# Expert outputs of a decoder layer added straight into the output tensor, with other tokens' rows for the spare places of a slot

## The reference, cut to what matters

```python
x = x + self_attention(layernorm(x))
x = x + cross_attention(layernorm(x), ctx)
# ffn on h = layernorm(x)
probs = softmax(h @ classifier_w.T)                 # 12 choices: 8 experts and 4 that return h
_, idx = top_k(probs + bias, 2)                     # two choices per token
rw = take_along_axis(probs, idx) * 1.5
for e in range(8):
    out += rw_e * ((silu(h @ gate_w[e].T) * (h @ up_w[e].T)) @ down_w[e].T)
out += h * sum(rw of the four others)
x = x + out
```

## Time and profile before

| what | us |
|---|---|
| median of 3 runs (2280.91 to 2284.15) | 2281.41 |
| the profiled execution, its own time | 2280.95 |
| its span, first to last instruction | 2279.2 |
| PE busy in the span | 2100.5 |
| DVE, ACT, POOL busy in the span | 1380.0, 946.2, 868.6 |
| 35 slots of `experts`, first instruction about 2027, to the end of the span | 252 |

### The profile page before, as it was taken

The page is one execution under the profiler, slowest core; times in us unless marked ns, Lnnn a source line. Parts: engine busy times, 40 slices in busy tenths (PEclk is TensorE's granted clock), DMA queues, the critical chain, the costliest instruction groups (busy, mean ns, idle before and its releaser), DMA issues. The chain is left out here.

```text
span 2279.2 us, 36906 instructions
## 1 busy us (share of the span) xinstructions
PE 2100.5 (92%) x10838; PEld 1693.3 (74%) x10839; DVE 1380.0 (61%) x3046; ACT 946.2 (42%) x2030; POOL 868.6 (38%) x977
## 2 busy tenths in 40 slices
PE   6899999987899997799999999999999799949994
PEld 6788888875777776588888888888887588824442
DVE  6455555557888886477677777777777556631110
ACT  4233333334232322365665665666565422213331
POOL 5100000002666666444433433443443256524552
PEclk9999999998999998899999999999999899969997
DMA  8212121146444444242222222222221284425555
GB/s 242 73 54 74 56 71 57 54 126 189 142 149 137 143 150 150 93 132 73 64 72 76 63 70 65 63 65 70 63 64 41 67 262 146 142 82 112 90 90 110
DMA packets 290938, 230.23 MB, mean 101 GB/s; under 512 B 150194, under 2 KB 257314, under 8 KB 288482
## 3 DMA queue, kind: packets, MB, share of 16 engines
q1 hardware_dynamic: 277122, 194.39, 29.0%
q0 software_dynamic: 8736, 18.39, 4.7%
q10 hardware_dynamic: 4992, 16.37, 2.2%
HBM read 140.30 MB, written 92.46 MB: 102 GB/s over the span
## 5 line engine op out<-in xcount | busy, mean ns | idle before, releaser
L2434 ACT ACTIVATE ca_prob<-ca_ps_s,ca_down,ca_scales 112x487 f32<-112x487 f32 x256 | 194.0, 758 | 243.2 <-DVE ca_down L2562 243.2
L2243 POOL TENSOR_TENSOR ca_k<-ca_k 125x512 f32<-125x512 f32 x64 | 83.1, 1298 | 326.1 <-DVE ca_k L2525 326.1
L2558 DVE TENSOR_REDUCE ca_top<-ca_ps_s 112x1 f32<-112x487 f32 x256 | 168.4, 658 | 42.6 <-PE ca_ps_s L77 42.6
L76 PE MATMUL out_ps_y<-out_w_lo,out_o_hi 128*128 128x512 f32 x448 | 178.6, 399 | 0.0
L645 POOL COPY sa_val<-lat_v 112x128 f32<-112x128 f32 (+1 forms) x64 | 19.6, 308 | 411.6 <-PE sa_ps_o L704 411.3
L75 PE MATMUL ca_ps_p<-ca_w_hi,ca_c_hi 128*125 128x512 f32 x384 | 157.2, 409 | 14.6 <-DVE ca_w_lo L2579 10.0
L75 PE MATMUL out_ps_y<-out_w_hi,out_o_hi 128*128 128x512 f32 x308 | 128.6, 418 | 37.9 <-DVE out_o_lo L1300 17.1
L2552 DVE TENSOR_TENSOR ca_pT_lo<-ca_ps_t,ca_pT_hi 125x448 fp32r<-125x448 f32 x256 | 152.7, 616 | 3.0 <-ACT ca_pT_hi L2442 3.0
L77 PE MATMUL ca_ps_p<-ca_w_hi,ca_c_lo 128*125 128x512 f32 x384 | 152.9, 398 | 0.0
L76 PE MATMUL ca_ps_p<-ca_w_lo,ca_c_hi 128*125 128x512 f32 x384 | 152.8, 398 | 0.0
L2333 PEld LDWEIGHTS ca_ps_t<-ca_ident,ca_prob 112*125 112x125 f32 x1024 | 132.3, 189 | 19.1 <-ACT ca_prob L2434 11.3
(11 more groups left out here) (299 smaller groups left out, 6074.1 us busy)
## 6 DMA issues: line engine op xcount, KB each, us to landing
self_outT<-sa_ov SPq DMA_DIRECT2D x64, 224.0 KB, 2.4
out_o_raw<-self_outT SPq DMA_DIRECT2D x56, 256.0 KB, 2.9
cross_qT<-out_qt SPq DMA_DIRECT2D x56, 256.0 KB, 2.4
ca_q_raw<-cross_qT SPq DMA_DIRECT2D x64, 224.0 KB, 2.8
cross_outT<-ca_ov SPq DMA_DIRECT2D x64, 224.0 KB, 3.0
out_o_raw<-cross_outT SPq DMA_DIRECT2D x56, 256.0 KB, 4.1
expert_raw<-in_expert_w SPq DMA_DIRECT2D x8, 1536.0 KB
ca_c_first<-in_ctxT SPq DMA_DIRECT2D x15, 750.0 KB, 5.2
```

The source lines that it names most:

```text
L76: pe.matmul(out, a_hi, b_lo, start=False, stop=False)
L2243: pool.tensor_tensor(k1[0:m, :], k1[0:m, :], k2[0:m, :], ALU.add).then_inc(k_added.sem, 1)
L2434: act.activation(prob[j % 2][:, 0:KV], ps_s[j % 2][:, 0:KV], ACT.Exp, bias=down[:, j:j + 1], scale=scales[par][:, n:n + 1], accum_out=tota ...
L2558: dve.tensor_reduce(top[:, j:j + 1], ps_s[j % 2][:, 0:KV], AX.X, ALU.max, negate=True).then_inc(topped.sem, 1)
```

## The change

The adds go straight to the output tensor `out`, where `cross_output` now also stores its rows. `rows_x`, its spare rows and the copy at the end are gone. `out` has no spare rows, so each spare place of a slot needs a real row that the slot doesn't hold (its addend is zero, but two addends of one DMA may not share a row). The numbers of these rows are computed per slot: DVE writes a 128x128 matrix of marks (`mark`, three instructions, for slot i+3 in step i), PE multiplies it with a column of ones into a new PSUM bank `ps_n` (in `turn_x`), and DVE turns the sums into row numbers (`name`, three instructions, for slot i+1 in step i, right behind `gate` of slot i). POOL's second conversion reads those numbers and waits for them. `turn_x` of slot n now waits for the marks of slot n and for the first instruction of `name` of slot n-1, since both use the one bank. `ps_a` gives up its second bank for it. Before the slots, POOL and DVE write seven small constants. On DVE, `name` of slot 0 stands behind `merge` of slot 4.

```diff
@@ cross_output, SP
-            sp.dma_start(rows_x[T:T + P, :], ahead_of.w_hi[:, 0, :].bitcast(F32)).then_inc(spare_put, 16)
...
-            sp.wait_ge(spare_put, 32)
+            sp.wait_ge(spare_put, 16)
@@ experts
-        ps_a = [ctx.bank(f"ps_a{i}", P, KI, P) for i in range(2)]
+        ps_a = ctx.bank("ps_a", P, KI, P)
+        ps_n = ctx.bank("ps_n", P, 1)
@@ SP
-            whole = lambda ap: ap.rearrange("(p n) d -> p (n d)", p=P)
             sp.wait_ge(put.sem, put.at(NU - 1))
-            sp.dma_start(whole(out), whole(rows_x[0:T, :])).then_inc(stored, 16)
-            sp.wait_ge(stored, 16)
@@ POOL
+            pool.iota(row_no_i[:, :], pattern=[[1, P]], base=0, channel_multiplier=0).then_inc(numbers, 1)
+            pool.iota(part_no_i[:, :], pattern=[[0, 1]], base=0, channel_multiplier=1).then_inc(numbers, 1)
+            pool.memset(ones[:, :], 1.0).then_inc(numbers, 1)
...
-                pool.tensor_copy(spot_i[i % 2][:, :], list_i[:, bass.ds(s, 1), 0]).then_inc(spotted.sem, 1)
+                wait(pool, named, s, 2)
+                carry(pool, h, ticks)
+                pool.tensor_copy(spot_i[i % 2][:, :], spot_f[:, bass.ds(s, 1)]).then_inc(spotted.sem, 1)
...
-                pool.indirect_dma_start(rows_x, bass.IndirectOffsetOnAxis(ap=spot_i[i % 2][:, 0:1], axis=0),
+                pool.indirect_dma_start(out, bass.IndirectOffsetOnAxis(ap=spot_i[i % 2][:, 0:1], axis=0),
@@ PE, turn_x
                 mm.then_inc(x_turned.sem, 1)
+                wait(pe, marked, n, 2)
+                if not isinstance(n, int) or n:
+                    wait(pe, named, n, -3)
+                pe.matmul(ps_n[:, :], missing[i % 4][:, :], ones[:, :], start=True, stop=True).then_inc(ranked.sem, 1)
@@ PE, turn
-                wait(pe, a_kept, n, -2)
+                wait(pe, a_kept, n, -1)
@@ DVE
+            def mark(h, i):
+                s = h * 4 + i
+                wait(dve, merged, s, 1)
+                carry(dve, h, ticks)
+                dve.tensor_copy(token[i % 4][:, :], list_i[:, bass.ds(s, 1), 0]).then_inc(marked.sem, 1)
+                wait(dve, marked, s, 0)
+                dve.tensor_tensor(bound[:, :], upper[:, :], token[i % 4][:, :], ALU.subtract).then_inc(marked.sem, 1)
+                wait(dve, marked, s, 1)
+                carry(dve, h, ticks)
+                dve.tensor_scalar(missing[i % 4][:, :], row_no[:, :], bound[:, 0:1], None, ALU.is_le).then_inc(marked.sem, 1)
+
+            def name(h, i):
+                s = h * 4 + i
+                t = token[i % 4][:, :]
+                wait(dve, ranked, s)
+                dve.scalar_tensor_tensor(other[:, 0:1], ps_n[:, :], spare_no[:, 0:1], t, ALU.add, ALU.subtract).then_inc(named.sem, 1)
+                wait(dve, named, s, 0)
+                dve.scalar_tensor_tensor(other[:, 1:2], t, float(T), other[:, 0:1], ALU.is_ge, ALU.mult).then_inc(named.sem, 1)
+                wait(dve, named, s, 1)
+                dve.tensor_tensor(spot_f[:, bass.ds(s, 1)], t, other[:, 1:2], ALU.add).then_inc(named.sem, 1)
...
             def step(h, i):
                 if has(h, i):
                     gate(h, i)
+                if has(h, i + 1):
+                    name(h, i + 1)
                 if has(h, i + LEAD):
                     merge(h, i + LEAD)
+                if has(h, i + 3):
+                    mark(h, i + 3)
...
-            for s in range(LEAD):
+            merge(0, 0)
...
+            for s in range(1, LEAD):
                 merge(0, s)
+                if s < 4:
+                    mark(0, s - 1)
+            name(0, 0)
```

More of the change, by code:

```diff
@@ L2617, in cross_attention, with experts @@
     return ctx
-def experts(nc, run, rows_n, rows_x, tokens, slots, experts_w, out):
+def experts(nc, run, rows_n, out, tokens, slots, experts_w):
     KI = INTER // P
@@ L2644, in experts @@
         list_i = sb("list_i", [P, NS, 2], I32)
+        token = [sb(f"token{i}", [P, 1]) for i in range(4)]
+        bound = sb("bound", [P, 1])
+        missing = [sb(f"missing{i}", [P, P]) for i in range(4)]
+        other = sb("other", [P, 2])
+        spot_f = sb("spot", [P, NS])
+        row_no_i, part_no_i = sb("row_number_i", [P, P], I32), sb("partition_i", [P, 1], I32)
+        row_no, part_no = sb("row_number", [P, P]), sb("partition", [P, 1])
+        upper, spare_no = sb("upper", [P, 1]), sb("spare_number", [P, 1])
+        ones = sb("ones", [P, 1])
         row_i = [sb(f"row_i{i}", [P, 1], U32) for i in range(4)]
@@ L2671, in experts @@
         y_free = ev("y_free", 1, 4)
-        stored = ctx.sem("stored")
+        numbers = ctx.sem("numbers")
+        marked = ev("spares_marked", 3)
+        ranked = ev("spares_ranked", 1)
+        named = ev("rows_named", 3)
         block = ctx.enter_context(nc.Block())
@@ L2788, in turn @@
                 wait(pe, gated, n)
-                wait(pe, a_kept, n, -2)
+                wait(pe, a_kept, n, -1)
                 for k in range(KI):
-                    mm = pe.transpose(ps_a[i % 2][:, k, :], a[i % 2][:, k * P:(k + 1) * P], ident[:, :])
+                    mm = pe.transpose(ps_a[:, k, :], a[i % 2][:, k * P:(k + 1) * P], ident[:, :])
                 mm.then_inc(turned.sem, 1)
@@ L2839, in keep @@
                 wait(act, down_mm, n, -2)
-                act.activation(aT[i % 2][:, :, :], ps_a[i % 2][:, :, :], ACT.Copy).then_inc(a_kept.sem, 1)
+                act.activation(aT[i % 2][:, :, :], ps_a[:, :, :], ACT.Copy).then_inc(a_kept.sem, 1)
             def copy_y(h, i):
@@ L2911, in build @@
     x1 = dram("x1", (T, D))
-    rows_n, rows_x = dram("x2_normed", (T + P, D)), dram("x3", (T + P, D))
+    rows_n = dram("x2_normed", (T + P, D))
     tokens = [nc.dram_tensor(f"tokens_of_experts{c}", (DUMP + P, 2), I32).ap() for c in range(2)]
@@ L2943, in build @@
         experts_w = ExpertWeights(nc, expert_w)
-        keep = run, rows_n, rows_x, tokens, slots, experts_w
+        keep = run, rows_n, out_rows, tokens, slots, experts_w
         with cross_out_w, experts_w.early:
@@ L2947, in build @@
         with experts_w.whole:
-            experts(nc, *keep, out_rows)
+            experts(nc, *keep)
 def layouts(x, ctx_2048, pos_BxS2, itok_BxS_4096_4607, L0_attn_q_proj_w, L0_attn_kv_a_proj_w, L0_attn_kv_a_ln_w,
```

7 lines of the change are left out of this document (added).

## The result

The changed kernel is slower: 2300.99 us median of 4 runs (2298.89 to 2302.43), against 2282.78 us (2280.91 to 2285.49) for the kernel before on the same chip. The ratio is 1.0084, 95% interval 1.0068 to 1.0099. I had forecast +6 us; it is +18. The profiled execution has a span of 2297.9 us, 18.7 more than before.

The account below looks back on a forecast made before the run. PE's slots, the last adds and the final copy were taken to set the end. Terms -13.4 + 5.6 + 15.1 - 1.1 = +6.2 us gave a forecast of 2287.5 us, range 2279 to 2296.

Parts of the forecast that it names:

- The stop of the sequencer: Steady slots: PE's sequencer stops before `project` until `name` begins; 6.33 us per slot, +0.52 each, +15.1 us.
- rival (c): Loop and first slots: longer path, 6.5 us per slot, clock lost in first gaps; up to +15 us, 2296; chance 0.13.
- Rival (a): PE slots: waiting product doesn't hold up the sequencer, number read meanwhile; sum -7.2 us, 2274; chance 0.12.
- The product as work: PE, each slot: the product with ones takes 0.19 us, by itself making a slot 6.00 instead of 5.81.
- The copy goes: End of kernel: removing the copy of `rows_x` to the output, with nothing beside it, saves 13.4 us.
- The start of `cross_output`: The spare rows' store there is one of many on SP, off every chain; removing it put at 0.
- The first slots: Head of experts stage: `project` of slot 0 waits behind late `name` of slot 0; +5.6 us by slot 4.
- The adds: Last adds: they ran 1.1 us late, which the slower pace takes up; -1.1 us.
- Two things that I put at 0: DVE's six small `mark` and `name` instructions fit its wait per slot; `ps_a` with one bank costs nothing.
- rival (d): Adds into `out` take longer, or DVE's new work holds up POOL; 1 us in all, no separate chance.

Follow-up runs that it names:

- number_first: Changed kernel, but PE reads the expert's number for `project` at the head of the step, ahead of the waiting product: 2280.53 us, ratio 0.9992.
- name_before_gate: Changed kernel, but on DVE `name` of slot i+1 stands ahead of `gate` of slot i: 2278.83 us, ratio 0.9991.
- behind_project: Changed kernel, but PE's product with ones and its waits stand behind `project` instead of ahead of it: 2277.25 us, ratio 0.9983.
- name0_early: Changed kernel, with `name` of slot 0 directly behind `mark` of slot 0 on DVE: 2297.02 us, ratio 1.0074.
- pool_waits: Changed kernel, with POOL also waiting for the last add's landing before its block ends: 2303.60 us, ratio 1.0103.
- before_no_copy: Kernel before without the copy at the end, base rows stored to `out`, the experts' part missing from the output: 2268.15 us, ratio 0.9953.
- after_again: The changed kernel measured once more, nothing altered: 2299.55 us, ratio 1.0080.
- lists_first: behind_project with two-byte marks, a POOL wait in `cross_output`, and the last two experts' weights loaded behind list 14: 2267.66 us, ratio 0.9939.
- spare_kept: Changed kernel with the store of 128 spare rows put back into `cross_output`, into a tensor nobody reads: 2295.39 us, ratio 1.0058.
- behind_half_spare: behind_project with two-byte marks and ones, and the spare rows' store kept in `cross_output`: 2273.01 us, ratio 0.9967.

## Why the prediction was wrong, step by step

The direction and the mechanism in the slots were right. The sum was not, and the time lies beyond the upper end of my range of 2279 to 2296. The span grew by 18.7 instead of 6.2. Of these 12.5 us the loop of the steady slots is 5.9, the end 2.8, the start of `cross_output` 3.0 (I had put it at 0) and the first slots 1.6; the last adds take 0.8 off.

**The stop of the sequencer, the main term: right in kind, 5.9 us too small.** The chain has `project` behind the read behind `name` behind the gate, and number_first and name_before_gate show that breaking it at either place restores PE's own pace. Two sizes were off. From the gate's end to `project` I had 0.10 + 1.28 = 1.38 and allowed 0.1 either way; it is 1.49, as in rival (c). Of these 0.11 the end of `name`'s first instruction is 0.03 (it takes 0.21 and not 0.16, and starts 0.08 and not 0.06 ahead of the gate's end), and the way from there to `project` is 0.08: 1.36 on the mean where I had 1.28. It is 1.36 in the loop and 1.30 in the step shown above, which stands behind the loop and has one register instruction less there. From the start of `project` to its gate's end I had 4.95 from the kernel before; it is 5.05, since with the small product directly ahead the second record of `project` comes 0.10 later. Together 0.20 x 29 = 5.9. I had taken the 4.95 as fixed though the change puts a new instruction right ahead of it. Where 29 slots share a term, 0.1 us is 3 us.

**Rival (a), the wait held in a queue.** It fell: the period is 6.53, and 6.0 only where the read doesn't stand behind a wait for the newest gate. The rule of the Trainium skill that I weighed ("Advanced Engine Details and Errata", Sequencer and Instruction Queues) would have made it 6.00 at once; the runs agree with the trace of before and not with the rule.

**The product as work**: 0.19 predicted, 0.17 measured in behind_project. Right.

**The copy goes: -13.4 predicted, -10.6 measured.** I took the copy's landing minus the add's, and said that nothing lies beside it. POOL's drain did, and it ended 2.9 us behind the last landing. It stood in the trace of before, and in its chain of waits, which ends with POOL's L2631 from 2260.43 on. My sentence that nothing stands behind the last landing was wrong by 3.1 us.

**The start of `cross_output`, put at 0**: the changed kernel loses 2.2 us there by the collision, or 0.9 where the clock holds. I called the store off every chain, and it is; but POOL's subtraction came earlier and fell onto DVE's. The load behind the store, issued 0.3 us earlier, is a part of that; with the store put back POOL is still 0.8 us earlier than in the kernel before, and why stays open. The other 0.8 of the +3.0 is in code that the change doesn't touch, and within what executions differ.

**The first slots: 5.6 predicted, 7.2 measured.** `project` of slot 0 came 6.0 later, counted from the last residual addition, where I had 6.3. Then slot 0 ran longer at 1.2 GHz (7.50 instead of 6.44 to the gate's end), and three steps were 6.58 instead of 6.3. The clock was in my rival (c) with 1.8 for each time; one of them came with 1.06. But the reason that I gave holds only in part: name0_early shows that without the late `name` the late list and the clock give the same 77. In pool_waits, with the same code, the clock fell once more, in slot 2, for 1.7 us, and `project` of slot 4 came at 78.45.

**The adds: -1.1 predicted, -1.9 measured.** The slower pace takes up all of their lateness, and the last three adds follow at 5.40 to 5.58 us where I had 5.7. Right in kind, but the size rests on single executions: against before_no_copy (24.75) the changed kernel's 23.58 is -1.2 and after_again's 24.03 only -0.7.

Two things that I put at 0 stayed there: DVE's six instructions per slot, and the one bank of `ps_a`, since behind_project has both and PE never waits. The landing of an add takes 4.5 to 5.1 us in `out` (4.7 to 5.5 in `rows_x`, once 6.05), apart from the two beside the weights in lists_first, and rival (d) did not show.

## What to carry to other kernels

A wait costs by what stands behind it in its engine's stream, not by its length. When an instruction with a new wait goes in, look for register reads behind it and put it where its release is already old: moving one product with its two waits took the ratio from 1.0080 to 0.9983 here, some 22 us. When a step at the end is taken away, list everything that it hid, the drains of the other engines too. When a DMA is taken out of a queue, the loads behind it come earlier (0.3 us here), so look at what the engines that they feed then run beside; a wait between the two instructions orders them, the DMA only shifted them.

## What the runs showed of the hardware

**DVE and POOL, both on SBUF, within 0.1 us of each other.** One of them runs its usual time and the other takes longer: DVE's 0.55 becomes 1.48 to 1.58 beside POOL's 1.26, and in spare_kept, where DVE is 0.10 ahead, POOL's 1.29 becomes 1.59. The Trainium skill ("SBUF — State Buffer", Summary: rules for kernel authors) says that the second of the two to issue is blocked until the first has finished, where DVE is in a mode that uses two ports or reads two operands from SBUF while POOL reads it. Whether DVE's instruction, which reads one, is in such a mode no row shows. The trace agrees on the order in nine of ten cases; in behind_half_spare POOL's record begins 0.04 behind DVE's and it is still DVE's that takes 1.58, so starts this close don't tell who was first.

**POOL's drain** takes 5.8 us after the last indirect DMA with nothing under way (pool_waits), and in the changed kernel no other engine's at the end takes more than 2.3 us (PE's, at 2279.5). What it does is open.

**A small 32-bit product directly ahead** of a chain of 512-column products makes the chain 0.08 to 0.10 us longer, all of it in the first one (second record 0.51 to 0.53 behind the first instead of 0.43).

**A register read behind a wait.** In the changed kernel PE's sequencer reads the expert's number 0.15 to 0.21 us behind the end of the instruction that releases the wait ahead of it, and the first product that uses the number follows 1.1 to 1.25 us behind the read's start.

**Two-byte operands** bring a product of 128x128 by one column from 0.17 to 0.06 us between other work (periods of 5.98 and 5.87 against 5.81).

Open: what the drain depends on, what made ACT's copy in `cross_output` 0.9 us earlier against the layer norm beyond what the store accounts for, and why the first 60 us of the program differ by up to 4 us between executions. None was tried.
